# Cross-attention's sums sent through DRAM, with the order of SyncE's queue and of the last projection changed

## The reference

```python
x = layernorm(x + self_attention(x))      # 16 heads of 16, causal
x = layernorm(x + cross_attention(x, ctx))  # see below
return ffn(x)                             # two quantised linear layers, 256 -> 1024 -> 256,
                                          # with silu, gelu and a layer norm between
```

```python
q, k, v = split_heads(Wq x + bq), split_heads(Wk c + bk), split_heads(Wv c + bv)
scores = rotary(q) @ rotary(k).T / sqrt(8)         # per head 256 x 256
out = softmax(scores) @ v                          # per head 256 x 8
return Wo @ out.reshape(b, 64, 256) + bo
```

## Time and profile before

| | |
|---|---|
| time, median of 3 runs | 563.03 us (562.54 to 566.03) |
| profiled execution | 563.8 us, of which the span is 561.9 us |
| TensorE busy | 450.6 us (80%) |
| VectorE busy | 442.4 us (79%) |
| ScalarE busy | 382.0 us (68%) |
| GpSimd busy | 289.6 us (52%) |
| DMA packets | 51674, 37.07 MB |
| mean granted clock of TensorE | 0.848 of full speed |

### The profile page before, as it was taken

How to read it: one execution, slowest core, us unless ns; L and a number is a source line. 1 busy time by engine, 2 the same in 40 slices (tenths; PEclk the granted TensorE clock), 3 DMA queues, 4 the chain that set the end, 5 groups by cost and what they waited for, 6 DMA issues and landing times. The chain is left out here.

```text
span 561.9 us, 12026 instructions
## 1 busy us (share of the span) xinstructions
PE 450.6 (80%) x4162; PEld 243.0 (43%) x4162; DVE 442.4 (79%) x965; ACT 382.0 (68%) x698; POOL 289.6 (52%) x387
## 2 busy tenths in 40 slices
PE   6568799999999999999999999889877701555563
PEld 5354545555545555555555555433333200333342
DVE  2656687888988979889889798865848959999973
ACT  2222266767767667676676686687767787999972
POOL 5742565447555574475555744620032727667652
PEclk9677799999999999999999999975987875555555
DMA  6134318233242242332422323210000000000010
GB/s 217 48 97 149 97 46 248 66 92 91 57 111 67 64 110 60 90 91 60 108 69 64 106 61 82 71 56 1 3 1 1 1 0 1 10 28 19 30 37 29
DMA packets 51674, 37.07 MB, mean 66 GB/s; under 512 B 21408, under 2 KB 47648, under 8 KB 51488
## 3 DMA queue, kind: packets, MB, share of 16 engines
q1 hardware_dynamic: 51328, 36.10, 22.8%
q10 hardware_dynamic: 288, 0.23, 0.2%
HBM read 24.52 MB, written 10.49 MB: 62 GB/s over the span
## 5 line engine op out<-in xcount | busy, mean ns | idle before, releaser
L970 DVE TENSOR_REDUCE MX<-mx_b 128x2 f32<-128x512 f32 x256 | 167.8, 679 | 37.6 <-PE mx_b L581 36.4
L775 ACT ACTIVATE PB<-e_b 128x512 f32<-128x512 f32 x256 | 149.6, 592 | 64.7 <-PE e_b L609 63.8
L581 PE MATMUL mx_b<-KA,QA 48*128 48x256 bf16 x512 | 100.8, 282 | 10.3 <-DVE MX L970 10.1
L609 PE MATMUL e_b<-QA,KA 50*128 50x256 bf16 x512 | 100.9, 281 | 2.7 <-ACT PB L775 2.1
L626 PE MATMUL u_b<-PB,VA 128*32 128x256 f32 x1024 | 86.2, 404 | 3.4 <-ACT PB L775 2.9
L897 POOL TENSOR_TENSOR SP<-SP,srec 128x1024 f32<-128x1024 f32 x15 | 28.5, 1901 | 79.0 <-DVE srec L942 79.0
L581 PEld LDWEIGHTS mx_b<-KA,QA 48*128 48x128 bf16 x512 | 30.1, 95 | 88.5 <-issue 48.9
L1238 POOL TENSOR_TENSOR H<-H,row_tab 128x1024 f32<-128x1024 f32 x16 | 37.8, 2359 | 22.9 <-ACT H L1196 19.5
L1285 PE MATMUL r_b<-identh,Q 128*128 128x128 f16 x128 | 16.6, 311 | 39.5 <-ACT Q L1206 39.5
L1291 PE MATMUL z_b<-w2q,Q2T 128*128 128x256 bf16 x128 | 30.2, 417 | 19.3 <-ACT Q2T L1217 19.3
L314 POOL TENSOR_TENSOR rs<-mv,epsc 128x1 f32<-128x1 f32 x32 | 6.1, 189 | 72.5 <-DVE mv L301 50.2
(11 more groups left out here) (169 smaller groups left out, 1048.4 us busy)
## 6 DMA issues: line engine op xcount, KB each, us to landing
KA<-parts_k SPq DMA_DIRECT2D x64, 96.0 KB
QA<-parts_q SPq DMA_DIRECT2D x64, 96.0 KB
parts_q<-part_q SPq DMA_DIRECT2D x32, 128.0 KB, 2.0
parts_k<-part_k SPq DMA_DIRECT2D x16, 192.0 KB, 2.1
C<-in_ctx SPq DMA_DIRECT2D x16, 128.0 KB, 3.0
X<-in_x SPq DMA_DIRECT2D x16, 128.0 KB, 2.9
out_y<-O SPq DMA_DIRECT2D x16, 128.0 KB, 1.7
XT<-in_xT SPq DMA_DIRECT2D x15, 128.0 KB, 2.2
```

The costliest lines, as they stand in the source:

```text
L581: m = nc.tensor.matmul(mx_b[n % 2][:, D * k:D * k + D], QA[low:low + K_MAX, 2 * i.ring + b, h, P * u:P * u + P], KA[low:low + K_MAX, 2 * i ...
L609: m = nc.tensor.matmul(e_b[n % 2][:, D * k:D * k + D], KA[low:low + K_EXP, 2 * i.ring + b, h, P * sc:P * sc + P], QA[low:low + K_EXP, 2 * ...
L775: nc.scalar.activation(PB[:, n % 4].rearrange("p e t -> p (e t)"), e_b[n % 2][:, :], ACT.Exp, scale=XC ** -0.5).then_inc(e_sb.sem, 1)
L970: nc.vector.tensor_reduce(MX[:, b, e, 2 * q:2 * q + 2, u], mx_b[n % 2][:, :].rearrange("p (e s) -> p e s", e=2), AXL.X, ALU.max).then_inc( ...
```

## The change

- The eight transposes of the sums, the reciprocals and products per image, the two transposes back and the copy with bias go away. In their place: `store_sums` writes `US` to DRAM (one DMA of 256 KB per image), `load_sums` reads the pair's sums back as 128 x 256 and its denominators as 128 x 32, `reciprocals` (VectorE) inverts the latter, `recip_out` writes them to DRAM, `recip_in` reads them back repeated for the 8 channels, and `means` (GpSimd) multiplies into `AT`.
- The input columns of `Wo` are reordered to fit; the values' bias goes through `Wo` once (`value_bias`, turn 0) and is added with the output bias.
- `x_out_proj`, `norm2` and what follows are done for `late`, pair i-2, at the same steps. In turn 15 they are done for pair 13 and pair 14.
- SyncE's turn starts with the second image's sums and the maxima rows for b = 1, then the key rows of pair j (until now of pair a at the end of the turn before), then the context load. The other new hops stand about half a turn apart.
- In turn 15 `mean_square`, `mean_power` and `factors` of the first group stand after pair 14's projection.
- `identb` is made by two copies of a half instead of one addition, and the last pair's steps in the second stage move to later turns.

```diff
@@ -273,27 +259,52 @@
+def store_sums(sp, i, b):
+    if has(i, 2):
+        sp.wait_ge(ld_uv, 16 * (i.v - 1))
+        sp.wait_ge(ld_us, 16 * (i.v - 1))
+    wait(sp, u_sb, i, b + 1)
+    sp.dma_start(u_hbm[i.p][:, :, b].rearrange("c j x -> j c x"), US[:].rearrange("p s t -> p (s t)")).then_inc(moved[b], 16)
+def load_sums(sp, i):
+    if has(i, 1):
+        wait(sp, at_sb, i.plus(-1), 1)
+    for b in range(2):
+        sp.wait_ge(moved[b], 16 * (i.v + 1))
+    flat = u_hbm[i.p].rearrange("c j b x -> c (j b x)")
+    sp.dma_start(S32[:], flat[XC:XC + 1].rearrange("c (r t) -> (c r) t", t=32)).then_inc(ld_us, 16)
+    sp.dma_start(UV[:], flat[0:XC].rearrange("c (r t) -> (c r) t", t=D)).then_inc(ld_uv, 16)
+def recip_out(sp, i):
+    wait(sp, u_rec, i, 1)
+    if has(i, 1):
+        sp.wait_ge(rec_in, 16 * i.v)
+    sp.dma_start(rec_hbm.rearrange("h (k t) -> (h k) t", t=32), S32[:]).then_inc(rec_out, 16)
+def recip_in(sp, i):
+    sp.wait_ge(rec_out, 16 * (i.v + 1))
+    sp.dma_start(RB[:], rec_hbm.unsqueeze(0).broadcast_to([XC, 16, D])).then_inc(rec_in, 16)
+def reciprocals(dve, i):
+    dve.wait_ge(ld_us, 16 * (i.v + 1))
+    nc.vector.reciprocal(S32[:], S32[:]).then_inc(u_rec.sem, 1)
+def means(pool, i):
+    pool.wait_ge(ld_uv, 16 * (i.v + 1))
+    pool.wait_ge(rec_in, 16 * (i.v + 1))
+    if has(i, 1):
+        wait(pool, xo_ps, i.plus(-1), 1)
+    nc.gpsimd.tensor_tensor(AT[:], UV[:], RB[:], ALU.mult).then_inc(at_sb.sem, 1)
...
+    nc.vector.scalar_tensor_tensor(out=Y2[:].unsqueeze(1), in0=g_b[g][:, 0:D].unsqueeze(1), scalar=xbo[:],
@@ -438,33 +449,48 @@
     def body(i):
-        nxt, j, a = i.plus(1), i.plus(2), i.plus(3)
+        prev, nxt, j, a = i.plus(-1), i.plus(1), i.plus(2), i.plus(3)
+        if real(prev):
+            store_sums(sp, prev, 1)
+        if real(i):
+            max_rows(i, 1)
+        if i.v == NPAIR - 1:
+            load_sums(sp, prev)
+            recip_out(sp, prev)
+            recip_in(sp, prev)
+        if i.v >= 0 and real(j):
+            expand_rows("k", j)
         if i.v >= 1 and real(a):
             load_c(a)
-        if real(i):
-            max_rows(i, 1)
         if real(a):
             cross_values(a)
         if real(j):
             store_parts("q", j)
+        if real(i):
+            store_sums(sp, i, 0)
+        if real(prev) and real(nxt):
+            load_sums(sp, prev)
         if real(nxt):
             max_rows(nxt, 0)
...
         if real(i.plus(4)):
             load_x(i.plus(4))
+        if real(prev) and real(nxt):
+            recip_out(sp, prev)
         if real(a):
             store_parts("k", a)
         if real(i.plus(5)):
             load_xT(i.plus(5))
+        if real(prev) and real(nxt):
+            recip_in(sp, prev)
         if i.v == 0:
             sp.dma_start(w1f[:].rearrange("p (k n) -> p k n", k=2), w1T.rearrange("(k p) n -> p k n", p=P)).then_inc(ld_ffn, 16)
             sp.dma_start(w2f[:].rearrange("p (k n) -> p k n", k=8), w2T.rearrange("(k p) n -> p k n", p=P)).then_inc(ld_ffn, 16)
-        if real(a):
-            expand_rows("k", a)
     prologue()
     bodies(sp, body)
+    store_sums(sp, Pair(0, NPAIR - 1), 1)
@@ -659,26 +691,24 @@
                 rotary_proj("q", g_b[1], j)
-            if s == 3 and real(prev):
-                u_transpose(pe, prev, 1, use(g_b[2], u_nrm, prev, 4))
             if s == 4 and fresh(a):
                 scores(a)
-            if s == 5 and real(prev):
-                att_transpose(pe, prev, use(g_b[2], at_sb, prev, 1))
             if s == 7 and real(nxt):
...
                 rotary_proj("k", g_b[2], a)
-            if s == 9 and real(prev):
-                x_out_proj(pe, prev, use(g_b[1], ln2, prev, 1))
+            if s == 9 and real(late):
+                x_out_proj(pe, late, use(g_b[1], ln2, late, 1))
+            if s == 12 and i.v == NPAIR - 1:
+                x_out_proj(pe, prev, use(g_b[2], ln2, prev, 1))
             if s == 10 and real(nxt):
...
                 transpose_p(a)
-            if s == 13 and real(i):
-                u_transpose(pe, i, 0, use(g_b[1], u_nrm, i, 2))
+            if s == 11 and i.v == 0:
+                value_bias(1)
             if s == 13 and real(a):
@@ -778,9 +808,9 @@
         if b == 1:
-            wait(act, ut_ps, i, 1)
+            act.wait_ge(moved[0], 16 * (i.v + 1))
         elif has(i, 1):
-            wait(act, ut_ps, i.plus(-1), 2)
+            act.wait_ge(moved[1], 16 * i.v)
         nc.scalar.activation(US[:].rearrange("p s t -> p (s t)"), u_b[:, :], ACT.Copy).then_inc(u_sb.sem, 1)
@@ -861,13 +889,16 @@
                 pt_copy(a)
-            if s == 13 and real(prev):
-                norm2(act, prev)
+            if s == (13 if real(nxt) else 12) and real(late):
+                norm2(act, late)
+            if s == (15 if real(nxt) else 12) and real(late):
+                square_sum(act, late)
             if s == 13 and real(a):
...
                 v_copy(i.plus(4), g_b[0])
-            if s == 15 and real(prev):
+            if s == 15 and i.v == NPAIR - 1:
+                norm2(act, prev)
                 square_sum(act, prev)
@@ -1025,20 +1061,23 @@
-            if s == 10 and real(prev):
-                norm2_stats(dve, prev, 1)
-            if s == 13 and real(i):
-                u_norm(dve, i, 0, 1)
-            if s == 14 and real(prev):
+            if s == 10 and real(late):
+                norm2_stats(dve, late, 1)
+            if s == 13 and i.v == NPAIR - 1:
+                norm2_stats(dve, prev, 2)
+            if s == 11 and i.v == 0:
+                value_bias()
+            if s == (14 if real(nxt) else 12) and real(late):
+                norm2_max(dve, late)
+            if s == 15 and i.v == NPAIR - 1:
+                factors(dve, 0)
...
-            if s == 4 and i.v == NPAIR - 1:
+            if s == 13 and i.v == NPAIR - 1:
...
-            if s == 11 and i.v == NPAIR - 1:
-                factors(dve, 0)
@@ -1114,11 +1153,17 @@
             split_parts(pool, nc.gpsimd, "q", j)
+        if real(late) and real(nxt):
+            means(pool, late)
         if real(a):
...
         if i.v == NPAIR - 1:
+            means(pool, late)
+        if real(late):
+            rstd(pool, ln2, late, mv2, rs2)
+        if i.v == NPAIR - 1:
+            means(pool, prev)
             mean_power(pool, 0)
-        if real(prev):
             rstd(pool, ln2, prev, mv2, rs2)
@@ -1249,9 +1292,11 @@
     mean_power(pool, 1)
+    means(pool, last)
     rstd(pool, ln2, last, mv2, rs2)
-    mean_power(pool, 2)
     for n in range(NPAIR):
+        if n == 5:
+            mean_power(pool, 2)
         wait(pool, qb, Pair(0, n), 1)
@@ -1291,12 +1336,9 @@
-    pe.wait_ge(s_tab, 3)
-    u_transpose(pe, last, 1, g_b[1])
+    pe.wait_ge(s_tab, 4)
...
-        if t == 2:
-            att_transpose(pe, last, g_b[0])
-        if t == 3:
+        if t == 6:
@@ -1385,25 +1427,29 @@
     for t in range(TURNS1):
-        if t == 1:
-            u_norm(dve, last, 1, 1)
+        if t == 2:
+            reciprocals(dve, last)
         if t == 4:
-            norm2_stats(dve, last, 1)
             factors(dve, 1)
         if t == 7:
+            norm2_stats(dve, last, 1)
+        if t == 10:
             norm2_max(dve, last)
...
             first_bias(i)
-        if t == 9:
+        if t == 13:
             factors(dve, 2)
...
 def _(sp):
+    load_sums(sp, last)
+    recip_out(sp, last)
+    recip_in(sp, last)
     for n in range(NPAIR):
```

More of the change, by code:

```diff
@@ L136, in build_layer @@
         ln1 = event("ln1", 7)
-        u_sb, ut_ps, u_nrm = event("u_sb", 2), event("ut_ps", 2), event("u_nrm", 4)
-        at_ps, at_sb, xo_ps = event("at_ps"), event("at_sb"), event("xo_ps")
+        u_sb, u_rec = event("u_sb", 2), event("u_rec")
+        at_sb, xo_ps = event("at_sb"), event("xo_ps")
+        s_bias_ps, s_bias = sem("s_bias_ps"), sem("s_bias")
+        u_hbm = [nc.dram_tensor(f"u_hbm{p}", (32, 4, 2, 2 * D), F32, kind="Internal").ap() for p in range(2)]
+        moved, ld_uv, ld_us = [sem(f"moved{b}") for b in range(2)], sem("ld_uv"), sem("ld_us")
+        rec_out, rec_in = sem("rec_out"), sem("rec_in")
+        rec_hbm = nc.dram_tensor("rec_hbm", (16, D), F32, kind="Internal").ap()
         ln2 = event("ln2", 7)
@@ L238, in tile_at @@
             return i.plus(n // 16), n % 16
[L241 to L255, removed]
         def x_out_proj(pe, i, ps):
@@ L259, in x_out_proj @@
             nc.tensor.matmul(ps[:, 0:D], xw["o"], AT[:, :], start=True, stop=True).then_inc(xo_ps.sem, 1)
[L261 to L266, removed]
         def square_sum(act, i):
@@ L629, in pv_quad, with value_bias @@
                 last.then_inc(pv.sem, 1)
+            def value_bias(g):
+                ps = use(g_b[g], Event(s_bias, 0), Pair(0, 0), 1)
+                pe.wait_ge(ld_cross, NCROSS)
+                nc.tensor.matmul(ps[:, 0:1], xw["o"], xb["v"], start=True, stop=True).then_inc(s_bias_ps, 1)
             def weight_total(g):
@@ L850, in body @@
```

(16 more changed lines are left out.)

48 lines of the change are left out of this document (20 added, 28 removed).

## The result

The changed kernel takes 572.74 us (median of 4 runs, 570.84 to 574.18) against 564.53 us for the kernel before (4 runs): the ratio is 1.0143, 95% interval 1.0085 to 1.0201. It is slower by 1.4%, where 551 was forecast: outside the range of 543 to 562, on the other side of no change. Its profiled execution took 570.84 us, span 568.7, against the 561.9 of before.

What follows compares the result with a forecast made beforehand. The prediction took TensorE and VectorE to bound about half the turn each. Its terms, mainly -14.2 us in turns 1 to 12 and +4.8 in the last turn, summed to -12.4: 551 us, range 543 to 562.

Steps and rivals of the forecast that it cites:

- the landing of the store from US: Each turn: the store lands before the next copy, half a turn later, against 2.1 us for the largest store; cost 0.
- The 1.18 us a turn: Steady turns: two removed groups of four transposes, 0.59 us each, come off the turn; bounds 0.59 and 1.55.
- rival (a): Steady turns: VectorE holds the turn more than read, only 0.59 us gained per turn, total 558; 15%.
- tight spot: Steady turns: context load, issued later, lands at 258.2 and TensorE wants it at 258.5; cost 0, bounds 0 and 0.5 a turn.
- the 20.4 forecast: Turn 13: 1.6 us less, 0.6 for the step-3 transposes and 1.0 for the step-13 ones at half clock.
- The store link: Last turn's serial chain: from copy done at 403.41 to store landed at 405.5.
- +4.8: Last turn: a serial chain of DMA hops, projection and norm delays the last copy by 4.8 us; bounds +3.5 and +6.5.
- Sums that take a store and a load (4.3 us): Second stage, turn 2: VectorE waits for them, against transposes removed; net -0.7 us, bounds -1.5 and +1.5.
- Rival (c): Steady turns: maxima rows land late behind a 256 KB store and two loads; 1.5 us beyond gives 571; 12%.
- Rival (b): Last turn into second stage: TensorE idles, half clock stays through the second stage's start, +4 us, 555; 10%.
- The +0.5 for the weights: Turn 1: the new hops queue behind 2 MB of weights, +0.5 us once; bounds 0 and 2.
- the 551.4 of the sum: Whole kernel: the profiled execution's 563.8 us less the summed 12.4 us.

Runs made afterwards that it cites:

- e1: The changed kernel with each 256 KB store of sums issued as four stores of 32 partitions, same bytes and addresses: 558.55 us, 0.9911 of the kernel before.
- f1: The changed kernel with four stores of 32 partitions per image and the context load ahead of the key expansions: 554.71 us, 0.9852 of the kernel before.
- e4: The changed kernel without any of the new DMAs, sums, denominators and reciprocals being constants: 549.98 us, 0.9756 of the kernel before.
- g1: The kernel before, with the changed kernel's one-piece 256 KB store per image added, its data never read: 597.29 us, 1.0603 of the kernel before.
- f4: The changed kernel with four-piece stores, context load first, and unread filler products on TensorE in turns 13 and 15: 557.26 us, 0.989 of the kernel before.

## Why the prediction was wrong

**The step that failed** is the landing of the store from US: "before the next copy, half a turn later, against the 2.1 us of the largest store now: 0". The same 2.1 us stand in the last turn's chain. The row was of another shape. The store took 5.9 us on four engines, and what was issued behind it landed late too. It was priced by its bytes, with the estimate of the Trainium skill (DMA: Bandwidth & Descriptors, the two cost components), 2.6 us, as a second opinion. The section gives its fit for DMAs issued by GpSimd, and neither row nor fit says how many engines carry the transfer. The dimension stood in the diff. That the store is the cause of the lost time as a whole is shown by e1, which changes nothing else. It came back in four places (us, one profiled execution each):

| stretch | after | e1 | f1 | e4 |
|---|---|---|---|---|
| to turn 13 | 352.66 | 348.93 | 344.95 | 345.44 |
| turn 13 | 24.95 | 20.19 | 22.78 | 20.77 |
| turn 14 | 21.69 | 21.48 | 21.52 | 21.20 |
| turn 15 | 21.66 | 19.82 | 19.18 | 18.55 |
| from the last copy on | 147.74 | 143.38 | 142.87 | 142.54 |

- **Steady turns.** The 1.18 us a turn from the removed products was right (e4: 21.33 from 22.49; rival (a) falls). Other transfers land late behind the store, and with the context load's tight spot that took 0.69 of it. The tight spot was named (landing at 258.2, wanted at 258.5) and priced at 0, with 0.5 as the bound. Even a landing near the 3.0 us assumed does not clear it: e1, whose context lands in 3.1, still waits 3.0 us in four turns, and f1 wins another 4 us up to turn 13.
- **Turn 13.** Not in the forecast at all: a load 1.22 us late there was followed by half rate 18 us early. With the store cut up the clock falls at about 365 and the turn takes 20.19 us, near the 20.4 forecast (e4, without hops: 20.77). f1's is 2.6 us longer; TensorE waits 1.35 us for query rows at 346.56 there, and the clock is at half rate from about 347 to 350. What made those rows late was not tried.
- **The last turn.** The store link was mis-sized: 5.97 instead of 2.1. A link was left out as well: GpSimd makes pair 13's norm factor ahead of pair 14's means, and it ends as the means start in the changed kernel (412.67 and 412.66), in e1 (402.20 and 402.16) and in e4, where no hop is left (397.70 and 397.65). That end comes 13.4 us after the turn's first copy in the changed kernel, 11.6 in e1, 10.3 in e4 and in f1; the clock fell to half rate there 1.5, 5.3, 10.9 and 12.3 us after that copy. So e1's gain of 1.8 us in this turn can't be put down to the store link alone. The means follow 3.1 us behind the issue of the broadcast load (409.52 to 412.66; in f1 3.2, there with GpSimd waiting), where I had 2.6; against that the power over 14 columns took 2.60 us, not 3.55. Without hops 4.4 us of loss remain, against +4.8 forecast with them. That the forecast comes near e1's +5.7 and f1's +5.1 is therefore luck in part: it had a like figure for other links.
- **Second stage.** "Sums that take a store and a load (4.3 us)" took 5.9 and 1.8; VectorE's wait of 5.56 holds TensorE for 3.44. In e1 the stretch is 1.6 us shorter than before. The clock differs too: it stays at half rate until about 438 in the changed kernel, 17 us after the last copy, against 9 us in e1 and 7 in f1. How much of the 4.4 us between the changed kernel and e1 is the late sums and how much the clock was not separated.

**Rival (c)** had the mechanism (rows of maxima behind a 256 KB store) and, at 12%, a time of 571. In the changed kernel the waits for the rows themselves cost 0.7 us in eleven turns, so it was not what made it slow, and that its 571 is near the 572.7 measured is luck; g1 shows the mechanism at the second image's rows. Rival (b), the clock: its condition came true, the half rate stayed through the second stage's start. As a cause of its own it falls, since e1 and e4 leave the products as they are and win 14 and 23 us. As a part of what the late store costs it stays open, in turn 13, in the last turn and in the second stage; f4's fillers cost too much of TensorE's time to settle it. The +0.5 for the weights and the rest of the sum can't be told apart within these runs.

With the store in four pieces and the context load first (f1) the profiled execution takes 553.5 us against the 551.4 of the sum: of the 12.4 us forecast 10.3 are there (8.3 by the medians, 554.7 against 563.0), with the order of the queue changed as well.

## What to carry to other kernels

Price a DMA by the number of engines that its two shapes let it use, before its bytes: read the slowest dimension of both sides from the code, and if it is small, cut the transfer so that each piece has a large one (32 here; two pieces with 2 made it worse). A DMA on few engines is also charged to its neighbours in the queue: look for a raised landing time of transfers that were not changed, and for a small DMA that takes as long as a large one. Where the profile gives no landing time for a transfer, look for a stretch where only it is in flight: who waits for it gives its time, and the DMA share gives its engines. When an engine's work moves to a later turn, look in each engine's order for what now stands ahead of the new chain.

## What the runs showed of the hardware

- A 256 KB store with slowest dimension 4: 5.9 us at a DMA share near 0.25. Two of 128 KB with dimension 2: 8.9 us together at 0.13. Four of 64 KB with dimension 32: 1.9 us each, all four in 3.1.
- Pieces of half the bytes (32 KB) land in 1.8 us instead of 1.9, and the kernel gains nothing: at this size the bytes cost next to nothing.
- 4 KB issued 1.1 us behind the slow store were there 5.8 us after their issue; a slow store twice a turn, which nobody reads, cost 34 us of 563; in four pieces it cost 3.6, with an interval that touches no change.
- Two steps of the last turn, TensorE's products waiting for ScalarE: 1.65 us at full clock, 2.31 at half.
